# Score matmuls one batch ahead in a fused two-layer transformer kernel: the causal attention of layer 0

## What is computed

```python
qf = taylor_exp(q)        # [1, x/d^(1/4), vec(x x^T)/(sqrt(2) sqrt(d))]
kf = taylor_exp(k)
A = jnp.tril(jnp.einsum('bhnf,bhmf->bhnm', qf, kf))
y = jnp.einsum('bhnm,bhme->bhne', A, v)
z = 1.0 / (jnp.einsum('bhlf,bhlf->bhl', qf, jnp.cumsum(kf, axis=2)) + EPS)
y = y * z[..., None]
```

## Time and profile before

| what | value |
|---|---|
| median of 3 runs | 5682.14 us (5677.97 to 5682.83) |
| the profiled execution | 5686.72 us, its span on the slowest core 5685.2 us |
| PE busy, matmuls | 2664.9 us, 47% of the span |
| DVE busy | 1596.1 us, 28% |
| ACT busy | 882.8 us, 16% |
| POOL busy | 288.3 us, 5% |
| spans of the 8 cores | 5664.3 to 5685.2 us |
| mean granted TensorE clock of the cores | 0.644 to 0.647 |

### The profile page before, as it was taken

One profiled execution on the slowest core, in us unless ns is written; L12 is line 12 of the kernel. 1 busy time (PEld: TensorE's weight loads), 2 busy tenths in 40 slices (PEclk: granted clock), 3 DMA queues, 4 the chain that ended last, 5 costly groups with the idle time before them and its releaser, 6 DMA issues. The chain is left out here.

```text
span 5685.2 us, 47783 instructions; the slowest of 8 cores (5664.3 to 5685.2 us)
## 1 busy us (share of the span) xinstructions
PE 2664.9 (47%) x16028; PEld 1344.1 (24%) x16028; DVE 1596.1 (28%) x3289; ACT 882.8 (16%) x1580; POOL 288.3 (5%) x475
## 2 busy tenths in 40 slices
PE   2554444444462999644443333333620466204544
PEld 1222222222341444311111222121310122101211
DVE  4121110100023111400022222222276555454333
ACT  1012222222201101100001222222010122100000
POOL 0100000000011202010000000000100000110000
PEclk9765555555565999777765555555655677556777
DMA  2200000000014726022210000000104201241112
GB/s 70 27 1 1 1 1 1 1 1 1 1 16 59 75 23 67 1 44 45 44 30 15 1 1 1 1 1 1 12 4 89 52 37 41 58 72 37 31 44 74
DMA packets 186073, 153.26 MB, mean 27 GB/s; under 512 B 108016, under 2 KB 151024, under 8 KB 183792
## 3 DMA queue, kind: packets, MB, share of 16 engines
q0 software_dynamic: 147200, 116.57, 13.7%
q1 hardware_dynamic: 38640, 33.64, 1.9%
HBM read 224.77 MB, written 25.17 MB: 44 GB/s over the span
## 5 line engine op out<-in xcount | busy, mean ns | idle before, releaser
L1547 PE MATMUL a0yp<-b1vaug,b1Bp 128*128 128x65 bf16 x2176 | 221.2, 234 | 644.7 <-ACT b1Bp L1597 334.3
L556 PE MATMUL g1hp<-b4q1T,b4tern 128*128 128x512 bf16 x1024 | 300.9, 466 | 214.9 <-ACT b4hsp L574 124.8
L1612 DVE TENSOR_TENSOR b1Bp<-b1Bp,b1tril 128x128 bf16<-128x128 bf16 x256 | 57.7, 225 | 1080.0 <-ACT b1Bp L1593 1079.3
L1537 PE MATMUL a0sb<-b1qTa,b1kTa 17*128 17x128 bf16 x2176 | 344.8, 301 | 1.7 <-PEq L1455 1.7
L1547 PEld LDWEIGHTS a0yp<-b1vaug,b1Bp 128*128 128x128 bf16 x2176 | 138.1, 116 | 791.4 <-issue 791.4
L1597 ACT ACTIVATE b1Bp<-a0sb 128x512 bf16<-128x512 f32 x384 | 229.3, 597 | 617.0 <-PE a0sb L1537 617.0
L556 PEld LDWEIGHTS g1hp<-b4q1T,b4tern 128*128 128x128 bf16 x1024 | 115.2, 115 | 400.2 <-issue 329.8
L207 PE MATMUL f0gps<-b2lnT,b2wg 128*128 128x512 bf16 x768 | 178.4, 386 | 64.3 <-DMA b2wu<-f0wu 62.1
L1537 PEld LDWEIGHTS a0sb<-b1qTa,b1kTa 17*128 17x128 bf16 x2176 | 183.5, 123 | 40.3 <-issue 2.1
L1124 ACT ACT_TABLE_LOAD x32 | 41.1, 1283 | 882.5 <-PE a1a0g0sl L1054 688.0
L214 PE MATMUL f0ups<-b2lnT,b2wu 128*128 128x512 bf16 x768 | 173.6, 379 | 0.0
(11 more groups left out here) (793 smaller groups left out, 4153.4 us busy)
## 6 DMA issues: line engine op xcount, KB each, us to landing
b4big<-g1w POOLq DMA_DIRECT2D x16, 1024.0 KB, 9.5
hs_scr<-b4hsp POOLq DMA_DIRECT2D x32, 512.0 KB, 2.9
b4big<-g1w POOLq DMA_DIRECT2D x64, 256.0 KB, 4.0
b4big<-hs_scr SPq DMA_DIRECT2D x64, 256.0 KB, 4.5
b2wg<-f0wg POOLq DMA_DIRECT2D x48, 256.0 KB, 4.5
b2wu<-f0wu POOLq DMA_DIRECT2D x48, 256.0 KB, 5.2
xs<-x SPq DMA_DIRECT2D x1, 8192.0 KB, 30.0
b3wbuf<-a1wq POOLq DMA_DIRECT2D x32, 256.0 KB, 4.3
```

Of the source, the lines that this page charges most:

```text
L556: mm = t.matmul(hp[:, c % 2, n4 * 512:(n4 + 1) * 512], t1v[:, j, c * 128:(c + 1) * 128], q1T[:, j, n4 * 512:(n4 + 1) * 512], start=(j == 0 ...
L1537: t.matmul(sbat[:, gb % 2, jj * 128:(jj + 1) * 128], kT[hb:hb + 17, oc, j * 128:(j + 1) * 128], qT[hb:hb + 17, oc, i * 128:(i + 1) * 128], ...
L1547: mm = t.matmul(yps[:, h, 0:65], Bp[:, gb % 2, jj * 128:(jj + 1) * 128], v_aug[:, j, 65 * h:65 * h + 65], start=first_av, stop=False)
```

## The change

The body of PE's loop is cut into two functions, `emit_s` for the waits and score matmuls of a batch and `emit_av` for its waits and products. Within a block all batches of all heads are put into one list, and PE issues the scores of a batch ahead of the products of the batch before it in the list; the last products of the block close it. ACT gets one wait more ahead of the ACTIVATE of a batch without a diagonal: `ph_s` must have counted all earlier batches. The buffers, the matmuls, the ACTIVATEs and DVE's part stay as they are.

```diff
-                for h in range(16):
-                    hb = 32 * (h % 3)
-                    oc = h // 3
-                    first_av = True
-                    for k, (j0, nj) in enumerate(bl):
...
+                nb_ = len(bl)
+
+                def emit_s(h, k):
+                    (j0, nj) = bl[k]
+                    gb = _bykey[(i, h, k)][5]
                     hb = 32 * (h % 3)
                     oc = h // 3
+                    if gb >= 2:
+                        t.wait_ge(ph_s, gb - 1)
+                    for jj in range(nj):
+                        j = j0 + jj
+                        t.matmul(sbat[:, gb % 2, jj * 128:(jj + 1) * 128],
+                                 kT[hb:hb + 17, oc, j * 128:(j + 1) * 128],
+                                 qT[hb:hb + 17, oc, i * 128:(i + 1) * 128],
+                                 start=True, stop=True).then_inc(ss_s, 1)
+
+                def emit_av(h, k):
+                    (j0, nj) = bl[k]
+                    gb = _bykey[(i, h, k)][5]
+                    t.wait_ge(ph_s, gb + 1)
+                    if i >= 1 and h == 0 and k == 0:
+                        t.wait_ge(nm_s, i)
+                        t.wait_ge(ca_s, i)
+                    for jj in range(nj):
+                        j = j0 + jj
+                        mm = t.matmul(
+                            yps[:, h, 0:65],
+                            Bp[:, gb % 2, jj * 128:(jj + 1) * 128],
+                            v_aug[:, j, 65 * h:65 * h + 65],
+                            start=(k == 0 and jj == 0), stop=False)
+                    mm.then_inc(ab_s, 1)
+                    if k == nb_ - 1:
+                        mm = t.matmul(yps[:, h, 0:65], tril[:, :],
+                                      v_aug[:, i, 65 * h:65 * h + 65],
+                                      start=False, stop=(i == 0))
+                        if i >= 1:
+                            mm = t.matmul(yps[:, h, 0:65], onescol[:, :],
+                                          ws["C_bf"][0:1, 65 * h:65 * h + 65],
+                                          start=False, stop=True)
+                        mm.then_inc(av_s, 1)
+
+                stream = [(h, k) for h in range(16) for k in range(nb_)]
+                for n, (h, k) in enumerate(stream):
+                    emit_s(h, k)
+                    if n >= 1:
+                        emit_av(*stream[n - 1])
+                emit_av(*stream[-1])
...
                 else:
+                    s.wait_ge(ph_s, gb)
                     s.activation(Bp[:, gb % 2, 0:128 * nj],
                                  sbat[:, gb % 2, 0:128 * nj],
                                  AF.Square).then_inc(ph_s, 1)
```

## The result

The changed kernel took 5143.9 us (median of 8 runs, 5135.9 to 5145.5) against 5682.5 us before (median of 10). The ratio of the means is 0.904, 95% interval 0.901 to 0.907; the medians are 539 us apart, where the prediction had 5147 us and 536 us less. The profiled execution took 5135.9 us. One further execution, in which the granted clock of four cores was 0.647 instead of 0.661, took 5220 us and is left out.

What follows compares the result with a forecast made beforehand. No engine bounds the stage, but one serial chain through PE, ACT and DVE does. Overlap saves 548 us, 12 is given back: 5686.7 - 536 = 5150.7 profiled, 5147 given by the median; 8-in-10 range 5110 to 5190.

Steps and rivals of the forecast that it cites:

- Two hops at a time: Hop: a batch's first score matmul to the next's; even and odd batches' hops overlap, 548 us less before 12 given back.
- The two sums: Time of all heads in the stage, 16 heads over 16 blocks: 1153 us before and 605 us after.
- filling and draining: Overlap stays within a block, so each of 16 blocks fills and drains once: 7 to 15 us, taken as 12.
- the table: Predicted head times by batches per head and diagonal batch's width, from 1.81 us undivided and 1.38 to 2.20 diagonal hops.
- The added wait: ACT's extra wait ahead of 384 ACTIVATEs without a diagonal: 0.06 us each, making that hop 1.87 us.
- N + D/2: Three batches per head: undivided batch's hop (N) plus half the head's last, diagonal batch's (D), 1.87 + D/2.
- PE's share: PE's work per undivided batch: 0.75 us, at most 0.81 with score-to-product changes, below the 0.935 available.
- drain rival (b): Products' weights load only after the last score matmul ends: PE period 1.02 us, 30 to 50 us, 5185; chance 0.10.
- signs of being wrong: In the new trace: products over 0.2 us after ACT's end, ACTIVATEs at a fixed gap, or clock 1.00.
- Rival (a): The clock rises in the stage as PE gets busier: 99 us less at most, 5050, or 5073; chance 0.07.
- (c): ACT's wait on its own previous ACTIVATE is dear, deciding from a 0.34 us gap; at 0.5, 5210; chance 0.04.
- (d): PE's writes and ACT's reads of sbat halves exclude each other: no overlap, 23 us more, 5705; chance 0.03.

Runs made afterwards that it cites:

- e4_three: The changed kernel with three halves of sbat and Bp instead of two and products two batches behind the scores; stage 656.9 us against 758.5.
- e1_wait_only: The kernel before with only the extra ACT wait on ph_s, old PE order kept; stage 1316.3 us against 1296.1, ratio 1.006.
- e3_split: The changed kernel without the extra ACT wait, masked batches raising their own semaphore pd_s; stage 750.6 us against 758.5.
- e5_short_act: The changed kernel with the ACTIVATE of every batch without a diagonal cut from 512 to 256 columns; stage 732.3 us against 758.5.
- e7_rows128: The changed kernel with score matmuls over all 128 rows instead of 17; stage 752.9 us against 758.5.

## Why the prediction was right

**Two hops at a time.** Right. The stage lost 537.6 us, the forecast was 548 - 12 = 536. A head of block 15 takes 4.06 us for 4.07. e4_three shows it from the other side: a third half brings 102 us more.

**The two sums.** Both were some 8 us too low, and the errors cancel, which is luck. The heads took 1160.6 us before, where I had 1153, and take 613.0 us, where I had 605: 547.6 less, for 548. The rest of the stage, what lies around the batches, went from 135.5 to 145.5 us. The 10 us more are what filling and draining gives back, for which I had 12. Before, every third head is 0.04 us longer than the table and a few single ones some 0.3. After, block 11 has the loop below, and in block 8 a head takes 2.62 to 2.67 us where the table has 2.56; the latter I can't explain.

**The added wait.** Right at 0.06 where the wait is long satisfied: e1_wait_only has 0.053 on a sole chain. In the new order, 10.5 us in the heads (e3_split) in place of 11.5.

**A bound that the prediction missed.** It said that with three batches a head costs N + D/2. For D of four tiles PE's order makes it D + 0.86 (e5_short_act), 3.06 and not 2.97. The changed kernel's own block 11 has this loop:

```profile
751.43 0.60 PE L1538 MATMUL a0sb<-b1qTa,b1kTa 17*128 17x128 bf16 x4
...
753.67 0.61 PE L1538 MATMUL a0sb<-b1qTa,b1kTa 17*128 17x128 bf16 x4
...
754.54 0.60 PE L1538 MATMUL a0sb<-b1qTa,b1kTa 17*128 17x128 bf16 x4
```

The scores of a D start at 751.43, those of the next head's second N, in the same half, at 753.67, and those of the next D at 754.54: 3.11 us for this head, 3.07 for two in three. Over 16 heads that is under 2 us. The miss is small only because N was long; with N of 1.66 the loop takes 9 of the 40 us.

**PE's share.** The new change from scores to products was put at 0.06 us at most, which was too low. Scores to products takes 0.53 us, not 0.49, and PE's batch 0.86 and not 0.81. It was still below 0.935, so the conclusion held. The drain rival (b) had 1.02: it is refuted by the 0.87 us of e4_three, and by products that start 0.06 us before the last score's end (1004.05 against 1004.11). One of the signs of being wrong that I had named did show, products later than 0.2 us after ACT's end: for the first N of the head above ACT ends at 1003.72 and the products start at 1004.05, because PE issues the scores at 1003.51 ahead of them. It costs nothing there, since the chain of that N has two N hops, 3.74 us, in 4.06.

**The clock.** Rival (a) fell: 0.50 in the whole window. But my reason for it, that PE still stops in every period for ACT, was not the right one. In e4_three PE runs without a gap for many batches and is busy 554 of 650 us, and the clock is 0.50 all the same:

```profile
325.00:975.00 650.00, 554.16 (x5232) 359.40 (x5232) 150.88 (x704) 334.59 (x641) 0.00 (x0) 0.50 0.01 2
```

What keeps it down in this stage, no run here shows.

**ACT and PSUM.** Rivals (c) and (d) fell. Two N ACTIVATEs stand 0.1 us apart where both have their scores (last section); (c) needed more than 0.34. And L1610 takes the 0.60 us of before beside PE's writes.

## What to carry to other kernels

When no engine is busy and every wait is of the next engine in a ring, measure one turn of the ring and count how many turns the buffers allow at a time: the time per batch is one turn divided by the number of buffers, until one engine's own sum is longer. The turn can be read from the serial trace before anything is changed; an engine's own sum only as far as its new neighbours in the queue cost nothing (here 0.81 was 0.86). Then walk the in-order queues once more for loops that mix a long turn with an engine's own work, since these appear only when the rest becomes short. A piece of work moved off the end of a stage into an engine that has become the bound is paid again there, with its changes of form.

## What the hardware showed that I had not expected

An ACTIVATE that waits for the one before it starts 0.2 us later than one that does not. It shows at a block's start, where the first two N have their scores while PE still waits for the running sums. Block 15 of the changed kernel, and of e3_split, which is without the wait:

```profile
998.00 1.29 ACT L1610 ACTIVATE b1Bp<-a0sb 128x512 bf16<-128x512 f32 x2 [7.83 <-PE a0sb L1538]
```

```profile
989.48 1.09 ACT L1619 ACTIVATE b1Bp<-a0sb 128x512 bf16<-128x512 f32 x2 [7.76 <-PE a0sb L1548]
```

One of them takes 0.597 us. So the second starts 0.1 us after the first one's end with the wait, and 0.1 us before it without. The Trainium skill ("ScalarE: Activation LUTs", section "What ACT_TABLE_LOAD costs") says that ACTIVATEs behind each other overlap by about 93 ns; the 0.1 us here are close to it. In the steady part of the changed kernel the N mostly wait longer for their scores, so that the 0.2 us are hidden.

A change between matmuls with few rows and with 128 costs PE about 0.12 us each way in this alternation (e7_rows128). No such cost shows between the closing matmul, which uses row 0 alone, and the 17-row scores behind it. Where the scores use rows from 32 or 64 on, both start within 0.01 us of each other; in every third head they use rows from 0 on and start 0.05 us later, as at 753.67 above.
